# A graph attention layer on one core: the heads' results accumulated transposed, normalised after they are copied out

## The reference

```python
h = (x @ W).reshape(N, H, C)
al_s = jnp.einsum('nhc,hc->nh', h, a_src)
al_d = jnp.einsum('nhc,hc->nh', h, a_dst)
e = jax.nn.leaky_relu(al_s[src] + al_d[dst], NEG_SLOPE)
m = jax.ops.segment_max(e, dst, num_segments=N)
ex = jnp.exp(e - m[dst])
denom = jax.ops.segment_sum(ex, dst, num_segments=N)
alpha = ex / (denom[dst] + 1e-16)
msg = h[src] * alpha[:, :, None]
out = jax.ops.segment_sum(msg, dst, num_segments=N)
...
h = jax.nn.elu(_gat_layer(x, src, dst, W1, att_src1, att_dst1, b1, concat=True))
out = _gat_layer(h, src, dst, W2, att_src2, att_dst2, b2, concat=False)
...
x = _layernorm(x + out)
```

## Time and profile before

| what | value |
|---|---|
| median of three runs | 962.7 us |
| the profiled execution | 957.08 us, its span 955.3 us |
| busy share of the span | PE 93%, DVE 64%, ACT 45%, POOL 26% |
| mean granted clock of TensorE | 0.981 of full |
| chain that ended last, by engine | PE 57%, DVE 17%, issue 9%, POOL 6%, ACT 5% |

### The profile page before, as it was taken

How to read it: one execution, slowest core, us unless ns; L and a number is a source line. 1 busy time by engine, 2 the same in 40 slices (tenths; PEclk the granted TensorE clock), 3 DMA queues, 4 the chain that set the end, 5 groups by cost and what they waited for, 6 DMA issues and landing times.

```text
span 955.3 us, 15152 instructions
## 1 busy us (share of the span) xinstructions
PE 886.1 (93%) x5719; PEld 799.3 (84%) x5719; DVE 609.2 (64%) x1137; ACT 425.2 (45%) x686; POOL 251.5 (26%) x166
## 2 busy tenths in 40 slices
PE   4998887999999999999999998989999999599996
PEld 2455555799888998889988897989999999599996
DVE  9547744747892798828897388673222344497887
ACT  5346534167643676337663385861111111387300
POOL 1000003049322363124621266500000000154452
PEclk9999997999999999999999999999999999889998
DMA  8508994652467234582164333456223431400223
GB/s 299 134 1 129 168 174 111 187 153 104 155 188 202 77 122 144 164 220 70 46 192 121 100 132 121 136 141 151 57 81 47 80 73 30 99 2 2 61 86 97
DMA packets 64451, 111.19 MB, mean 116 GB/s; under 512 B 31772, under 2 KB 33464, under 8 KB 63004
## 3 DMA queue, kind: packets, MB, share of 16 engines
q1 hardware_dynamic: 64379, 110.22, 44.4%
HBM read 85.25 MB, written 24.94 MB: 115 GB/s over the span
## 4 chain that ended last, share of the span: by engine, by line
PE 57%; DVE 17%; issue 9%; POOL 6%; ACT 5%; SPq 2%; DMA 2%; DVEq 1%; POOLq 0%; ACTq 0%
PE ps L1679 16%; PE ps L1681 16%; PE ps L1680 16%; POOL pbuf L586 4%; DVE pbuf L599 4%; PE ps L1710 3%; PE ps L1651 2%; DVE vbuf L1411 2%; DVE PTlo L613 2%; PE ps L1800 2%; SPq L656 2%; PE ps L1641 1%; DVE vbuf L1404 1%; DVE h2f L1590 1%; DMA w1raw<-in_L_gnn_W 1%
## 5 line engine op out<-in xcount | busy, mean ns | idle before, releaser
L586 POOL TENSOR_TENSOR pbuf<-pbuf,grow 125x625 f32<-125x625 f32 x100 | 167.3, 1674 | 525.1 <-ACT pbuf L571 225.3
L1679 PE MATMUL ps<-hx,PThi 125*125 125x260 f32 (+5 forms) x800 | 229.0, 286 | 9.4 <-DVE vbuf L1405 6.3
L1681 PE MATMUL ps<-hx,PTlo 125*125 125x260 f32 (+5 forms) x800 | 226.8, 284 | 0.0
L1680 PE MATMUL ps<-hlo,PThi 125*125 125x260 f32 (+4 forms) x800 | 226.5, 283 | 0.0
L1679 PEld LDWEIGHTS ps<-hx,PThi 125*125 125x125 f32 x800 | 150.5, 188 | 13.8 <-issue 6.8
L1680 PEld LDWEIGHTS ps<-hlo,PThi 125*125 125x125 f32 x800 | 150.9, 189 | 1.4
L1681 PEld LDWEIGHTS ps<-hx,PTlo 125*125 125x125 f32 x800 | 150.7, 188 | 0.0
L599 DVE SCALAR_TENSOR_TENSOR pbuf<-pbuf,counts 125x625 f32<-125x625 f32 x100 | 113.6, 1136 | 24.5 <-ACT pbuf L593 24.4
L1679 PE MATMUL ps<-W2p,hT 128*125 128x384 f32 x320 | 109.8, 343 | 3.2 <-DVE hT L1417 1.7
L608 ACT ACTIVATE PThi<-pbuf 125x625 fp32r<-125x625 f32 x80 | 58.0, 725 | 123.0 <-DVE pbuf L599 64.7
L1681 PE MATMUL ps<-W2p,hT 128*125 128x384 f32 x320 | 108.2, 338 | 0.0
(11 more groups left out here) (186 smaller groups left out, 1658.4 us busy)
## 6 DMA issues: line engine op xcount, KB each, us to landing
xr<-xT_scratch SPq DMA_DIRECT2D x30, 750.0 KB, 4.8
nbm<-mask_scratch SPq DMA_DIRECT2D x40, 273.4 KB
hidden_scratch<-vbuf SPq DMA_DIRECT2D x40, 224.0 KB
hblk<-hidden_scratch SPq DMA_DIRECT2D x10, 896.0 KB
xT_scratch<-xa SPq DMA_DIRECT2D x20, 375.0 KB, 10.8
w1f<-in_L_gnn_W SPq DMA_DIRECT2D x12, 512.0 KB, 9.4
w1raw<-in_L_gnn_W SPq DMA_DIRECT2D x4, 1536.0 KB, 7.8
w2raw<-in_L_gnn_W SPq DMA_DIRECT2D x14, 384.0 KB, 5.8
```

The lines of the kernel that those rows point to most:

```text
L586: pool.tensor_tensor(pslot(c), pslot(c), src[:, g * GN:(g + 1) * GN], ALU.add).then_inc(e_done, 1)
L1679: pe.matmul(dst, ahi, bhi, start=start, stop=False, skip_group_check=shared)
L1680: pe.matmul(dst[:, 0:n], ahi, blo, start=False, stop=False, skip_group_check=shared)
L1681: return pe.matmul(dst, alo, bhi, start=False, stop=stop, skip_group_check=shared)
```

## The change

In `chunk` the sides are exchanged: h is now the stationary side, 128 channels at a time (four tiles t), and the probabilities are the moving side. The result of a group comes out transposed, channels by destinations, in tiles of 128 x 626 or 128 x 624 (the groups are now 626 and 624 destinations, GW). A tile is cut into 370 columns, alone in its bank, and 256 (or 254), two tiles to a bank. The columns of ones are gone. Instead GpSimd keeps a running sum of the probabilities over a group's ten blocks (`add_up`, nine additions into `acc`), ScalarE and VectorE split that sum into two parts (`split_den`), and TensorE adds it over the 125 partitions with a stationary side of ones, which also spreads it over all partitions (`denominators` on TensorE, four matmuls). VectorE adds 1e-16 and takes the reciprocal of 626 columns.

The results are copied out of PSUM raw, the 370 columns by ScalarE (`evict_big`), the others by VectorE (`evict_small`). In the chunks that follow VectorE multiplies each tile by the reciprocals (`normalise`), ScalarE takes the exponential with the bias, which is now a column, and VectorE finishes the ELU in two instructions instead of one. A buffer of probabilities is free for its next chunk only when GpSimd has added it too.

The hidden array is stored transposed, 128 channels by 626 nodes a tile. A node block is loaded as 128 x 16 runs of 125 values, `transpose_h` is gone, and `split_hT` reads SBUF in one piece of 1000 columns per half. In the second group of heads 0 to 2 `make` for block 0 moves behind chunk 1.

```diff
...
+GW = (626, N - 626)
...
+BIG = 370
+SMALL = 256
+ITEMS = ((0, 0), (1, 0), (0, 1), (1, 1), (2, 0), (3, 0), (2, 1), (3, 1))
...
             if c >= PR:
                 act.wait_ge(pt_lo, c - PR + 1)
+                if c - PR < CHUNKS:
+                    act.wait_ge(pa_done, added_at(c - PR))
...
-                for lo, hi in RP:
-                    sp.dma_start(hblk[lo:hi, b % 2, :], hid_d[b * B + lo:b * B + hi, :]).then_inc(ld_hb[b % 2], 16)
+                sp.dma_start(hraw[:, b % 2, :, :], hidT_d[:, :, b * B:(b + 1) * B].rearrange("k p n -> p k n")).then_inc(ld_hb[b % 2], 16)
...
+            def add_up(c):
...
+                pool.wait_ge(pc_done, c + 1)
...
+                pool.tensor_tensor(acc[:, 0:w], pslot(c - 1) if b == 1 else acc[:, 0:w], pslot(c), ALU.add).then_inc(pa_done, 1)
...
             for c in range(CHUNKS):
                 h, g, b = chunk_of(c)
+                if b > 0:
+                    add_up(c)
                 if c + 2 < CHUNKS:
                     pool_add(pool, c + 2)
...
+            def denominators(q):
...
+                dve.wait_ge(den_ps, q + 1)
...
+                dve.tensor_scalar(rdt[:, 0:w], den_at(0, w), 1e-16, None, ALU.add).then_inc(d_eps, 1)
+                dve.wait_ge(d_eps, q + 1)
+                dve.reciprocal(rdt[:, 0:w], rdt[:, 0:w]).then_inc(d_done, 1)
...
+                dve.tensor_tensor(vT[q % 2][:, t, 0:w], vT[q % 2][:, t, 0:w], rdt[:, 0:w], ALU.mult).then_inc(u_done, 1)
...
+                dve.tensor_scalar(ebuf[:, 0:w], ebuf[:, 0:w], 1.0, -1.0, ALU.min, ALU.add).then_inc(e1_done, 1)
+                dve.wait_ge(e1_done, n + 1)
+                dve.scalar_tensor_tensor(u, u, b1c[:, k:k + 1], ebuf[:, 0:w], ALU.add, ALU.max).then_inc(hid_done, 1)
...
                 if b == 0 and c >= NB:
-                    evict_group(c // NB - 1)
-                if 3 <= b < 3 + GT and c >= NB:
-                    elu(GT * (c // NB - 1) + b - 3)
+                    evict_small(c // NB - 1, 0)
+                    evict_small(c // NB - 1, 1)
+                    split_den(c // NB - 1)
+                if c >= NB and b == (3, 1)[g]:
+                    denominators(c // NB - 1)
+                if c >= NB and 0 <= b - (4, 2)[g] < 2:
+                    normalise(c // NB - 1, 2 * (b - (4, 2)[g]))
+                    normalise(c // NB - 1, 2 * (b - (4, 2)[g]) + 1)
+                if c >= NB and 0 <= b - (6, 4)[g] < TH:
+                    elu(c // NB - 1, b - (6, 4)[g])
...
+                for t, small in ITEMS:
+                    lo, hi = (BIG, GW[g]) if small else (0, BIG)
...
+                    last = products(acc_at(t, small, g), ((hx[:, b, t * 128:(t + 1) * 128], hlo[:, b, t * 128:(t + 1) * 128]),
+                                                          (hi_slot(c)[:, lo:hi], lo_slot(c)[:, lo:hi])),
+                                    b == 0 and (not small or t % 2 == 0), b == NB - 1, True)
...
+                for lo, hi in ((0, BANK), (BANK, w)):
+                    pe.matmul(den_at(lo, hi), one_r[:, 0:1].broadcast_to([B, 128]), dhi[:, lo:hi], start=True, stop=False)
+                    t = pe.matmul(den_at(lo, hi), one_r[:, 0:1].broadcast_to([B, 128]), dlo[:, lo:hi], start=False, stop=True)
...
                 chunk(c)
-                if g == 1 and h + 1 < H:
+                if c >= NB and b == (2, 0)[g]:
+                    denominators(c // NB - 1)
+                if g == 1 and h + 1 < H and b > 0:
+                    if b == 1:
+                        make(h + 1, 0)
                     make(h + 1, b)
-                if c == CHUNKS - 3:
-                    transpose_h(0)
...
                 mm_half(2 * b)
                 if b == 0:
-                    pe.wait_ge(v_done, H * NB)
-                    transpose_h(1)
-                if b + 1 < NB:
-                    transpose_h(2 * b + 2)
+                    denominators(NG - 1)
                 mm_half(2 * b + 1)
-                if b + 1 < NB:
-                    transpose_h(2 * b + 3)
```

More of the change, by code:

```diff
@@ L492, in all_stored @@
         def all_stored(eng, j):
-            eng.wait_ge(hid_stored[j % GT], RS * (NG - 1 + j // GT))
+            for i in range(1 if j < GT else 2):
+                eng.wait_ge(hid_stored[i], 16 * TH * H)
         def win_bank(w):
@@ L757, in _ @@
                 if h > 0:
-                    for t in range(GT):
-                        store_hid(NB * h - GT + t)
+                    for t in range(TH):
+                        store_hid(2 * h - 1, t)
                 load_drow(h + 1, 0)
@@ L778, in _ @@
                 load_w2(c)
-            for t in range(GT):
-                store_hid(NB * (H - 1) - GT + t)
+            for t in range(TH):
+                store_hid(NG - 3, t)
             for c in range(6, 12):
@@ L783, in _ @@
             sp.wait_ge(mx_done, H * NB)
-            for t in range(GT):
-                store_hid(NB * (H - 1) + t)
-                if 1 <= t < 3:
-                    load_hb(t - 1)
+            for t in range(TH):
+                store_hid(NG - 2, t)
+            load_hb(0)
+            load_hb(1)
             sp.wait_ge(w2_lo_p, 7)
@@ L791, in _ @@
             load_w2(12)
-            sp.wait_ge(v_done, H * NB)
             load_w2(13)
             load_w2(15)
-            for t in range(GT):
-                store_hid(H * NB - GT + t)
+            sp.wait_ge(den_ps, NG)
             sp.wait_ge(pt_lo, CHUNKS)
@@ L824, in _ @@
             load_hb(2)
+            for t in range(TH):
+                store_hid(NG - 1, t)
+            all_stored(sp, NB - 1)
             for b in range(M2):
@@ L1147, in _ @@
             split_hT(0)
+            for t in range(TH):
+                evict_big(NG - 1, t)
+            act.wait_ge(pt_lo, CHUNKS)
+            act.wait_ge(pa_done, (NB - 1) * NG)
+            split_hT(1)
             act.wait_ge(ag, ag_at(CHUNKS - 1))
@@ L1163, in _ @@
                 split_w2(c)
+            split_hT(2)
+            for t in range(TH):
+                exp_of(NG - 1, t)
             def row2_out(to, banks):
@@ L1381, in _ @@
             dve_counts(dve, 1)
-            def denominators(q, part):
-                lo, hi = ((0, 2), (2, GT))[part]
-                n = GT * q
-                dve.wait_ge(ag, ag_block(q, hi - 1))
-                first = lo * BANK + in_bank(lo) - 1
-                step = BANK + in_bank(1) - in_bank(0)
-                sums = PS[0:B, :, :].rearrange("p k n -> p (k n)")[:, first:first + (hi - lo - 1) * step + 1:step]
-                dve.tensor_scalar(deps[:, n + lo:n + hi], sums, 1e-16, None, ALU.add).then_inc(d_eps, 1)
-                dve.wait_ge(d_eps, 2 * q + part + 1)
-                dve.reciprocal(rden[:, n + lo:n + hi], deps[:, n + lo:n + hi]).then_inc(d_done, 1)
-                dve.wait_ge(d_done, 2 * q + part + 1)
```

336 lines of the change are left out of this document (182 added, 154 removed).

## The result

The changed kernel takes **1157.6 us** (median of four runs, 1155.0 to 1158.4), the kernel before 962.7: a ratio of 1.2022, 95% interval 1.2006 to 1.2037. The forecast was 1013 us, in a range of 975 to 1045. The sign was right, the size was not: +195 us in place of +51.

The account below looks back on a forecast made before the run. It took GpSimd and VectorE taking turns at SBUF to bound first-group stages, TensorE the second groups of heads 0 to 2. Terms summed to +50.9 us on 957.1: 1008.0, so 1013 for the median, range 975 to 1045.

Parts of the forecast that it names:

- head 0, first group: Running sums added to GpSimd's turns: six chunks 1.2 us longer each, three others 0.6 each, sum +9 us.
- heads 1 and 2, first group: TensorE waits for the reciprocal, then five chunks run in GpSimd's and VectorE's turns: 52.1 us against 36.74, +15.4 each.
- head 3, first group: As in heads 1 and 2, with four W2 remainders 0.55 us dearer each: 54.3 us against 40.85, +13.4.
- head 3, second group, and the product's start: No 512-column matmuls to hide work, +12.6 us; second layer's product starts 5.1 us after the last chunk, +3.5.
- product: Second layer's product without its 160 TensorE transposes: 172.6 us against 187.2, -14.6.
- Matmuls: Shorter chunks, added sums and earlier evictions in the second groups of heads 0 to 2: together -3.8 us.
- 13 us a stage that turns could cost: Second groups of heads 0 to 2: loss if GpSimd and VectorE always took turns, three times; forecast took none.
- The wait before chunk 10: TensorE's 2.25 us wait before chunk 10 mostly goes because evictions start earlier: -2 us.
- The running sums: GpSimd's nine more adds per group of ten chunks, counted at 1.2 us each in turn with VectorE.
- rival of hidden sums: Running sums fit beside ScalarE without delaying VectorE, 1.2 us off each add on the path: 978 us, chance 0.14.
- The reciprocal: VectorE's reciprocal of 626 columns takes 4.9 us; TensorE stands still 3.4 us before the fifth chunk.
- rival of +45 us: TensorE's clock drops to 1.2 of 2.4 GHz in all starved chunks, 6.9 us each: 1058 us, chance 0.08.

Follow-up runs that it names:

- e2: Changed kernel with SyncE's mask loads issued earlier and the shift row's store and load put ahead of x blocks 8 and 9: 1035.2 us.
- e5: Kernel of e2 with GpSimd's running sums left out but for the first add of each group: 980.6 us.
- e6: Kernel of e2 with the reciprocal of 626 columns replaced by a one-column instruction and the sums by a constant: 1024.4 us.
- e4: Kernel before with only SyncE's list put in the changed kernel's order, masks and shift row later: 1088.6 us.
- e8: Kernel of e2 with VectorE's remainder of h moved right behind its chunk's counts in the second-group stages: 1040.9 us.

## Why the prediction was wrong, point by point

Between the profiled executions (1156.3 and 955.3 us of span) the forecast's terms came out so:

| term | forecast | measured |
|---|---|---|
| head 0, first group | +9 | +11.0 |
| heads 1 and 2, first group | +15.4 each | +15.3, +13.2 |
| head 3, first group | +13.4 | +12.2 |
| head 3, second group, and the product's start | +12.6 +3.5 | +10.6 |
| product | -14.6 | -12.2 |
| **second groups of heads 0 to 2** | **-3.8** | **+144.9** |
| before the first chunk, after the product | 0 | +5.9, +0.1 |

*The step that failed* stands under "Matmuls" and is the -3.8 for the second groups of heads 0 to 2: GpSimd's and VectorE's new work "lie beside TensorE's 77", and of the 13 us a stage that turns could cost, "I take none". It compared busy times. The change had also moved SyncE's mask loads and the shift row behind loads that wait for TensorE. In this list one wait held up all entries behind it, and the forecast followed none of these loads through it. Undoing that order alone gives 122 us (e2); the part that was named, the turns between GpSimd and VectorE, is the other 23, inside the bound of 3 x 13 (21 of them are the sums, e5).

*The wait before chunk 10*, of which the forecast took off 2 us, grew from 2.25 to 4.77 us, and it lies in the +11.0 of head 0's first group. ScalarE's copy out of PSUM (L1145) ends it; without the sums it is 1.23 us (e5).

```profile
256.95 0.65 PE L1750 MATMUL ps<-PThi,hx 125*128 125x370 f32 x1 [4.77 <-ACT vT L1145]
```

*The running sums*: right in kind: 5.5 to 10.8 us a group in the stages without blocks of h, against 7.2 to 9. The rival of hidden sums falls.

*The reciprocal*: 4.05 us against 4.9, and TensorE's wait of 2.1 before the fifth chunk against 3.4, as named. But that it lay on the path with its length is wrong: removing it gives 0.3 to 2.2 us in the groups that have one. The parts of the forecast for head 1's first group came out near (17.9 us to the fifth chunk, 30.4 for five chunks, 3.8 for the last; measured 16.8, 30.2 and 5.1), and so did their sum. That is luck in part: by the same sum the stage without the reciprocal would last 52.1 - 3.4 = 48.7 us, and e6 takes 51.0. So the turns between GpSimd and VectorE seem to fill the stage with or without it. The estimate by the Trainium skill's repeat count (VectorE: DVE Perf Modes, "First, the fixed hardware budget") of 5.2 us was too high as well; the trace decides, 6.5 ns a column.

*The product*: halves 8.44 us apart without transposes, as forecast. Its load was hidden: TensorE stood idle for 0.2 us before it (1.56 before the change), so of +12.6 and +3.5 for head 3's second group and the product's start came +11.9 and -1.4. The 2.5 us taken for a store had no row behind it; the changed kernel's stores of 313 KB landed 5.3 us after their issue (median). A wait of 3.5 us before the fourth half, behind the last reciprocal and normalisations, was not forecast; e6, without the reciprocal, has none, and its product takes 170 us.

```profile
874.55 0.68 PE L1750 MATMUL ps<-W2p,hT 128*125 128x384 f32 x1 [3.52 <-DVE hT L1491]
```

*TensorE's clock*: the dips came, behind waits (0.82 to 0.87 granted in the second groups of heads 0 to 2 and the first groups of heads 1 to 3). In the second groups they go with the ring (0.95 to 0.98 in e2). In the first groups at least half of each stays (0.90 to 0.93 in e2), and yet these stages last as forecast without a term for the clock; the rival of +45 us did not come.

*Before the first chunk*: this start lies between 201.3 and 209.3 us in the profiles of these twelve kernels, and at 206.7 in e4, whose prologue is that of the kernel before, so the 5.9 us are scatter for the most part.

## What to carry to other kernels

When a change reorders an engine that only issues DMAs, go through its list entry by entry: for each, what the entry ahead waits for, and whether the engine that releases this wait is itself waiting for what stands behind. Busy shares can't show such a ring; idle time before an instruction that reads a loaded tile ("issue") with the issues bunched right behind another engine's end can. And a wait that is seen in a trace is worth its length only if nothing uses the time beside it: run the kernel once without that instruction before counting it.

## What the runs showed of the hardware that was not expected

A VectorE instruction with a single input in SBUF was stretched beside GpSimd as well. In e8 the ELU's first step, 0.48 us with nothing beside it, beside a running sum of GpSimd (both rows):

```profile
283.05 1.53 POOL L953 TENSOR_TENSOR acc<-acc,pbuf 125x624 f32<-125x624 f32 x1 [4.49 <-DVE pbuf L626]
...
283.49 1.44 DVE L1486 TENSOR_SCALAR ebuf<-ebuf 128x626 f32<-128x626 f32 x1
```

The forecast had counted it at 0.5 us in turn. What differs is who begins first: in e2 three of the 32 rows of this step are stretched (1.57 to 2.13 us), and in these GpSimd's instruction had begun before it; in 22 others GpSimd's began 0.15 or 0.16 us behind it, and it took 0.47 or 0.48 us. The reciprocal of 624 columns, also with one input, took 4.05 to 4.07 us everywhere and did not slow GpSimd's instructions beside it (1.26 us for a W1 remainder, 1.30 in the earlier trace rows with nothing beside it).
